# Row statistics of the last 16 tiles moved to ScalarE in an attention layer that streams a 64 MB adjacency matrix

## What is computed

```
h      = relu(layernorm(x))                 # per row: (x - mean) / sqrt(var + 1e-5)
H      = h @ W_fc + b_fc
score  = (H @ a_src)[:, None] + (H @ a_dst)[None, :] + b_att,  -1e9 where adj == 0
out    = x + softmax(score, axis=1) @ H
```

## Time and profile before

| what | value |
|---|---|
| median of 3 runs | 187.31 us (187.17 to 188.09) |
| the profiled execution, its own time | 186.87 us |
| its span, first to last instruction | 185.1 us |
| TensorE busy | 159.5 us, 86% |
| VectorE busy | 132.6 us, 72% |
| ScalarE busy | 63.7 us, 34% |
| DMA | 71.64 MB, mean 387 GB/s |
| granted TensorE clock, mean | 0.972 |

### The profile page before, as it was taken

How to read it: one execution, slowest core, us unless ns; L and a number is a source line. 1 busy time by engine, 2 the same in 40 slices (tenths; PEclk the granted TensorE clock), 3 DMA queues, 4 the chain that set the end, 5 groups by cost and what they waited for, 6 DMA issues and landing times.

```text
span 185.1 us, 2660 instructions
## 1 busy us (share of the span) xinstructions
PE 159.5 (86%) x866; PEld 114.6 (62%) x866; DVE 132.6 (72%) x424; ACT 63.7 (34%) x136; POOL 9.5 (5%) x33
## 2 busy tenths in 40 slices
PE   0509689999955799999999999999999999999970
PEld 0307456675632686867768676686876866877740
DVE  0599999989796996978665487696773625459941
ACT  2353170703604963222232422442242424021020
POOL 2103201300003020000000000000000000000000
PEclk9999969999999799999999999999999999999996
DMA  5999999999999999999999999999999999997112
GB/s 171 384 441 427 425 428 432 430 421 436 420 428 418 439 425 425 436 421 426 420 423 428 428 425 423 425 425 425 426 422 425 438 422 421 418 395 272 70 60 58
DMA packets 8370, 71.64 MB, mean 387 GB/s; under 512 B 929, under 2 KB 1698, under 8 KB 3490
## 3 DMA queue, kind: packets, MB, share of 16 engines
q1 hardware_dynamic: 7776, 71.18, 91.9%
q10 hardware_dynamic: 578, 0.26, 0.6%
HBM read 69.34 MB, written 2.10 MB: 386 GB/s over the span
## 4 chain that ended last, share of the span: by engine, by line
PE 51%; DVE 21%; DMA 21%; ACT 2%; issue 2%; SPq 0%; DVEq 0%
PE bank L807 21%; PE bank L813 19%; DMA ring<-adj 17%; PE bank L831 6%; DVE mask L463 5%; DVE low L486 4%; DMA x_sb<-x 4%; PE bank L855 3%; DVE mask L472 3%; ACT weighted L359 2%; PE bank L845 1%; DVE stats L480 1%; DVE x_sb L594 1%; DVE low L574 1%; DVE x_sb L601 1%
## 5 line engine op out<-in xcount | busy, mean ns | idle before, releaser
L807 PE MATMUL bank<-mask,high 128*128 128x512 f32 x256 | 79.4, 412 | 14.3 <-DVE mask L472 6.9
L463 DVE TENSOR_SCALAR mask<-ring 128x1024 fp32r<-128x1024 int32 (+2 forms) x66 | 59.6, 920 | 29.5 <-DMA ring<-adj 18.2
L813 PE MATMUL bank<-mask,low 128*128 128x512 f32 x256 | 76.4, 401 | 0.0
L807 PEld LDWEIGHTS bank<-mask,high 128*128 128x128 f32 x256 | 47.2, 193 | 33.8 <-issue 8.7
L813 PEld LDWEIGHTS bank<-mask,low 128*128 128x128 f32 x256 | 49.7, 194 | 11.0
L405 ACT ACTIVATE mask<-ring,half_steep 128x512 fp32r<-128x512 int32 x43 | 28.8, 718 | 58.7 <-DMA ring<-adj 38.8
L831 PE MATMUL bank<-mask,w_cols 128*32 128x512 bf16 x256 | 20.3, 402 | 0.0
L371 ACT ACTIVATE relu<-x_sb,neg_mean 128x128 f32<-128x128 f32 x32 | 9.8, 390 | 13.3 <-DVE neg_mean L495 13.3
L831 PEld LDWEIGHTS bank<-mask,w_cols 128*32 128x32 bf16 x256 | 5.9, 96 | 11.4 <-issue 7.2
L480 DVE BATCH_NORM_STATS2 stats<-x_sb 128x6 f32<-128x128 f32 x32 | 7.2, 280 | 6.7 <-DMA x_sb<-x 6.7
L359 ACT ACTIVATE weighted<-relu,w_over_std 128x128 f32<-128x128 f32 x32 | 10.1, 391 | 3.3 <-DVE w_over_std L563 3.2
(11 more groups left out here) (80 smaller groups left out, 61.7 us busy)
## 6 DMA issues: line engine op xcount, KB each, us to landing
ring<-adj SPq DMA_DIRECT2D x18, 2048.0 KB, 16.2
ring<-adj SPq DMA_DIRECT2D x16, 1536.0 KB, 12.5
ring<-adj SPq DMA_DIRECT2D x3, 1024.0 KB, 9.1
out<-x_sb SPq DMA_DIRECT2D x7, 256.0 KB, 13.4
x_sb<-x SPq DMA_DIRECT2D x1, 1024.0 KB, 20.3
ring<-adj SPq DMA_DIRECT2D x4, 256.0 KB, 16.7
x_sb<-x SPq DMA_DIRECT2D x2, 256.0 KB, 5.4
x_sb<-x SPq DMA_DIRECT2D x1, 512.0 KB, 9.8
```

Source lines behind the costliest of these rows:

```text
L463: nc.vector.tensor_scalar(mask[:, n % MASKS, 0:cols], ring[:, n // 2 % RING, begin:begin + cols], 0.0, None, ALU.is_gt).then_inc(masks_rea ...
L807: nc.tensor.matmul(bank[:, b, :], high[:, t, :], mask[:, n % MASKS, cols], start=(t == 0), stop=False)
L813: last = nc.tensor.matmul(bank[:, b, :], low[:, t, :], mask[:, n % MASKS, cols], start=False, stop=(t == T - 1))
```

## The change

- VectorE's first chain of deviations covers tiles 0 to 7 at once (`SPANS`); tiles 8 to 15 keep a chain on VectorE; the four stages of scores and weights stay as they are. SyncE issues the first two loads of x ahead of the first halves of adj.
- For tiles 16 to 31 ScalarE makes the negative means (`late_means`: a copy with scale -1/128 and its accumulator output) and the sums of squared deviations (`late_squares`: a square with the mean as bias and its accumulator output). Each writes 128x128 into `low` or `high` beside the one column that is wanted. VectorE's 16 `bn_stats`, its steps on the halves and the first steps of the chain for these tiles are gone; the chain waits for all 16 squares.
- Dots go into the gaps of their own chain: dots 0 to 3 into the first, 8 to 15 into the second, and dots 16 to 23 with the quarters of mask 12 into the third; dots 24 to 31 follow it.
- Masks are put in another order: 8 to 11 ahead of the third chain, 13 behind the scores of stage 3, 14 to 19 between the splits.

More of the change, by code:

```diff
@@ new lines, in late_means @@
+            def late_means(t0, t1):
[5 more added lines that the diff above has]
+            def late_squares(t0, t1):
+                for t in range(t0, t1):
+                    act.wait_ge(late_means_ready, t - LATE + 1)
+                    nc.scalar.activation(high[:, t, :], x_sb[:, t, :], ACT.Square, bias=neg_mean[:, t:t + 1],
+                                         accum_out=var[:, t:t + 1]).then_inc(squares_ready, 1)
@@ L374, in _, with row_weights_of @@
+            def row_weights_of(k):
+                tiles = slice(*STAGES[k])
+                act.wait_ge(d_ready, k + 1)
+                nc.scalar.activation(w_j[:, tiles], d_raw[:, tiles], ACT.Exp, bias=minus_bound[:]).then_inc(w_ready, 1)
+            act.wait_ge(means_ready, 1)
+            relu_tiles(0, 4)
             act.wait_ge(v_in_psum, 1)
             nc.scalar.copy(v_rows[:].rearrange("p c d -> p (c d)"), ps_v).then_inc(v_rows_ready, 1)
[L376 to L391, removed]
@@ new lines, in _ @@
+            relu_tiles(4, 8)
+            row_weights_of(0)
+            act.wait_ge(w_over_std_ready, 1)
+            weigh(0)
+            weigh(1)
+            take_high(0)
+            weigh(2)
+            take_high(1)
+            act.wait_ge(lines_in_psum, 1)
+            nc.scalar.copy(lines[:], ps_lines).then_inc(lines_ready, 1)
+            take_high(2)
+            row_weights_of(1)
+            act.wait_ge(w_over_std_ready, 2)
+            weigh(3)
+            take_high(3)
+            late_means(16, 20)
@@ new lines, in _ @@
+            act.wait_ge(means_ready, 2)
[12 more added lines that the diff above has]
+            row_weights_of(3)
+            act.wait_ge(w_over_std_ready, 4)
+            for u in range(6, 10):
+                weigh(u)
+                if u > 6:
+                    take_high(u - 1)
@@ L608, in _ @@
             dve.wait_ge(x_landed[0], 16)
-            for t in range(0, 4):
+            for t in range(0, 8):
                 last = stats_of(t)
@@ L615, in _ @@
             nc.vector.tensor_scalar(minus_bound[:], dst_square[:], -HALF_NORM, -HALF_NORM, ALU.mult, ALU.add)
-            scores(0, dot_of(3))
-            mask_quarter(0, 0)
+            scores(0)
+            mask_quarter(0, 1)
             row_weights(0)
-            mask_quarter(0, 1)
             mask_quarter(0, 2)
+            mask_quarter(0, 3)
             split(0)
-            mask_quarter(0, 3)
             split(1)
-            deviations(1, between_1)
+            mask_unit(1)
+            split(2)
             for t in range(4, 8):
@@ L627, in _ @@
             scores(1, last)
[L628 to L632, removed]
+            mask_unit(2)
             row_weights(1)
@@ L636, in _ @@
             mask_unit(4)
+            for t in range(8, 16):
+                last = stats_of(t)
+            link(last)
+            link(sum_of_halves(1))
+            negative_mean(1).then_inc(means_ready, 1)
             mask_unit(5)
-            deviations(2, between_2)
+            deviations(1, between_1)
             scores(2)
```

78 lines of the change are left out of this document (24 added, 54 removed).

## The result

| what | before | changed |
|---|---|---|
| median (7 runs each, on the same chip) | 187.47 us (187.17 to 188.09) | 186.41 us (186.06 to 186.62) |
| ratio | | 0.9938, 95% from 0.9922 to 0.9954 |
| profiled execution, its own time / span | 186.87 / 185.1 us | 186.51 / 184.7 us |
| VectorE busy, instructions | 132.6 us, 424 | 127.2 us, 374 |
| ScalarE busy, instructions | 63.7 us, 136 | 74.5 us, 200 |

The change makes the kernel 0.6% faster, 1.06 us. The forecast was "no change" at 187.3 us: that is wrong. The time lies 0.01 us inside the lower end of the range, 186.4, which is luck.

A forecast was written before the change was run, and what follows sets the result against it. Bound: the landing of units 64 and 65, set by bytes, then 21 us of gapless TensorE. Terms 0 + 0 - 0.12 + 0 gave 186.75 for an execution like the profiled one, 187.3 as median (no change); range 186.4 to 188.8.

The forecast's parts named there:

- The bound: End of the kernel: landing of units 64 and 65 at 154.91, plus 1.3 us, 21 us of TensorE, last rows.
- That landing is a matter of bytes: Landing of units 64 and 65: DMA engines always full at 427 GB/s, bytes ahead unchanged, so loads cost 0.
- One of the signs that I had named for being wrong: Landing of units 64 and 65 moved by more than 1 us with the DMA engines full all along.
- TensorE tied with the landing: At unit 64 TensorE came 0.12 us ahead of the mask, so its earlier work gains at most 0.12 us.
- ScalarE's price: Tiles 16 to 31 on ScalarE: a mean costs 0.40 us and a square 0.50, accumulator read taken as 0.2.
- S: When ScalarE's 16 squares for tiles 16 to 31 are done: 46.6 us, bounds 44.1 to 48.9.
- From S to the end of units 16 to 19: Relus, dots, masks, then TensorE's denominators: done 22.6 us after the squares, at 69.2, 2.2 us ahead of 71.44.
- Lead isn't passed on, lateness is: TensorE leaving units 16 to 19 before 71.44 gains at most 0.12 us; leaving later costs nearly all of it.
- Start, tiles 8 to 15, loads: Three terms worth 0 each: TensorE begins within about 1 us of before; loads cost something past about 50 us.
- ScalarE's chain too long: Slower rival: accumulator reads from 0.31 us delay the squares past 48.9; at 0.42 the time is 189.6; chance 0.11.
- The gain gets through: Faster rival: landings not the bound, TensorE's 2.2 us at unit 16 come off the end, 185.1; chance 0.07.
- The clock: Slower rival: TensorE idles 2.2 us ahead of its last 21 us, slowed clock costs 1.7 us, 189.0; chance 0.04.

The follow-up runs named there:

- experiment 3: The changed kernel without the 12 low-part matmuls of tiles 21 to 23 in group 0: 186.43 us, ratio to before 0.9949.
- experiment 11: The changed kernel with 8 more unused squares on ScalarE ahead of the 16 that count: 186.47 us, ratio to before 0.9951.
- experiment 2: The kernel before without the 12 low-part matmuls of tiles 21 to 23 in group 0: 187.46 us, ratio to before 1.0001.
- experiment 1: The kernel before, unchanged, timed and profiled again: 187.38 us, ratio 0.9997.
- experiment 5: The changed kernel with 52 one-column memsets on VectorE, four a unit at units 40 to 52: 187.31 us, ratio to before 0.9983.
- experiment 6: The changed kernel with 26 one-column memsets on VectorE, two a unit at units 40 to 52: 186.44 us, ratio to before 0.9943.
- experiment 7: The kernel before without the 28 VectorE multiply-adds of row_sum for tiles 4 to 31: 186.99 us, ratio to before 0.9972.
- experiment 10: The kernel before with 36 one-column memsets on VectorE in place of the 28 row_sum multiply-adds: 187.61 us, ratio to before 1.0025.
- experiment 8: The kernel before with only the first two loads of x put ahead of the first halves of adj: 187.31 us, ratio 0.9982.
- experiment 12: The changed kernel with the first loads of x and adj in the order of before: 186.36 us, ratio to before 0.9948.
- experiment 4: The changed kernel with 16 more unused squares on ScalarE ahead of the 16 that count: 188.12 us, ratio to before 1.0038.
- experiment 9: The kernel before without the 28 row_sum multiply-adds and without the 12 low-part matmuls of tiles 21 to 23: 186.32 us, ratio 0.9940.

## Why the prediction was wrong

**The bound: right.** A landing ahead of group 2 ends the wait, with the DMA engines full at 427 GB/s throughout, and 21 us of gapless TensorE stand behind it. Experiments 3 and 11 confirm it for the changed kernel and experiment 2 for the one before.

**"That landing is a matter of bytes": the step that failed.** From it the sum took 0 for the landing. The bytes are the same and the landing came 1.18 us earlier than in experiment 1 and 0.61 earlier than in the profile of before, since its time is that of the bytes plus the lag of the last share, and each of VectorE's instruction fetches ahead of it puts 0.9 to 1.0 us on that lag; the change took one of them out (experiments 5, 6, 7 and 10). The number was in front of me: 0.95 us between 145.37 and 154.91 that the bytes did not explain. I called it unevenness and supposed that the order of the first loads may move it; experiments 8 and 12 say it does not. Looking at the queues in those 9.5 us would have shown the one packet that wasn't adj. Since I had kept it as an uncertainty of 0.95 us, the range just held, by 0.01 us and by luck; the chances did not. One of the signs that I had named for being wrong came true: a landing moved by more than 1 us, measured from experiment 1, with the DMA engines full.

**TensorE tied with the landing: true of one execution.** In the profiled execution it came 0.12 us ahead of the mask, in experiment 1 it waited 0.29. That execution was quicker than all seven timed ones beside it; VectorE's share began in it with a lag of 1.16 us, less than in any other of the 14 profiles (1.33 to 2.28). I built a sum of hundredths on it. The conclusion stood, that an earlier TensorE brings almost nothing as long as the landing stays. But with the landing 1.2 us earlier, TensorE's time counts: it would have ended last, as in experiment 7, and about half the gain would have been lost. So the change needs both of its effects: the fetch, and some of TensorE's 5.1 us.

**ScalarE's price: right in kind, too high in size.** The read of the accumulator lasts 0.19 us but adds only 0.09 to the distance: means 0.29 us apart and squares 0.39, where I took 0.40 and 0.50. By the formula of the Trainium skill (ScalarE: Activation LUTs, section What ACT_TABLE_LOAD costs) they would be about 0.20 and 0.29 apart without the read; the difference to what is measured is again the 0.09, for which the page has no figure. The last five means begin at 35.23, not 36.6, and S came at 42.9 instead of 46.6; the lower end of my bounds gave 44.1.

**From S to the end of units 16 to 19: right, 0.8 us short.** Scores at S + 6.3 (49.19; forecast S + 6.2), TensorE done at S + 23.4 (66.30; forecast S + 22.6). With S itself 3.7 us early, the lead at unit 16 was 5.1 us instead of 2.2.

**Lead isn't passed on, lateness is: right.** The wait of 0.70 at unit 30 and 0.71 at unit 64 show the lead lost; experiment 11 gives 4.6 us of it away for nothing; experiment 4 ends 1.07 us behind before at unit 16 and 0.74 us behind it in time, although its mask 64 began 1.1 us earlier than in experiment 1.

**Start, tiles 8 to 15, loads: right, worth nothing.** The first matmul came at 12.18 instead of 14.15, 2 us earlier where I had said within 1, and none of it is left at unit 30. The loads run dry when S passes 50, I said; in experiment 4 S was 49.24 and they had just done so.

**The rivals.** ScalarE's chain too long: no; experiment 4 shows the mechanism with its price, and experiments 11 and 4 put the point from which it costs between 4.6 and 6.2 us of TensorE's time at unit 16 from where the change left it. The gain gets through: the sign was right and the mechanism wrong, 1.06 us instead of 2.2, and not TensorE's. The clock: granted 1.00 in the 21 us of group 2, so it did not occur.

**Settled by the shares.** That a fetch delays one share, that a load has landed with its last share, and that the lag stays while the DMA engines are full, is what the 16 times of each load show in all 14 profiles. Fetches put down to ScalarE (8192 bytes) moved one lag by 0.65 to 0.70 us where they can be told apart from TensorE's, those of TensorE (16384 bytes) by 1.4 to 1.6 us. They do cost a landing something where their share becomes the last: TensorE's at 65.5 us in before put 0.45 us on all landings until VectorE's share overtook it again. What decides mask 64 is how often one and the same share is hit: VectorE's is hit three times behind 20 us in before, and TensorE's four fetches from 65 to 133 us hit four different ones. The profiles of before and changed differ by 0.4 us at mask 10 (40.08 in experiment 1, 39.68 changed), but there another share is the last, at 1.95 and 1.59 us, and VectorE's overtakes it; that difference is no part of the 1.18 us.

**Open.** Why a packet of 8192 bytes, whose record lasts 0.325 us, costs its share 1 us, and ScalarE's of the same size 0.7, is not settled, nor why the lags begin where they do. That a share is the work of one of the 16 DMA engines is inferred; the trace has no name of an engine. That a packet belongs to VectorE rests on the counts, and now also on its hitting the same share each time. The Trainium skill (Runtime: NRT & Kernel Launch, section Instruction fetch mechanics) has each sequencer fetch its own instructions by DMA in blocks of 16 KiB at a cost "mostly hidden"; the packets of q8 agree with the size, those of q14 are half of that, and with full DMA engines experiments 5 and 6 put 0.87 us on one of them, so here the measurement decides.

No version was faster than the changed kernel: experiments 3, 9 and 12 lie within 0.1 us of it.

## What to carry to other kernels

- Where loads bound a kernel with full DMA engines, follow the landings one by one. An interval that is longer than its bytes is a term of the sum and not noise; look at what else is in the queues there. Two causes can fall into one interval: where the trace gives the shares of a load, follow each share's lag and not the last one alone. Count instructions as well as busy time: 26 tiny ones cost nothing and 52 cost 0.9 us, because a fetch slid in front of the last landing that counts.
- When two things end at nearly the same time, one alone brings little and both together bring all (0.0, 0.55 and 1.03 us here). Test them apart and together.
- Compare the profiled execution with the timed runs before building on its tenths; where it lies outside of them, its ties may not be typical.

## What the runs showed of the hardware that was not expected

- With the DMA engines at a share of 1.01, each instruction fetch of 8192 bytes put down to VectorE delayed one and the same of a load's 16 shares by 0.9 to 1.0 us, for this and all later loads, and left the other 15 where they were; the landing moves by as much as that share gets behind the last of the others (0.2 to 1.0 us in the fetches from 50 us on).
- Fetches put down to ScalarE (8192 bytes) cost another share 0.65 to 0.70 us, those of TensorE (16384 bytes) 1.4 to 1.6 us; most of them never show in a landing.
- The lags begin anew when the loads run dry: in experiment 4 the last was 1.89 us ahead of a stretch with a DMA share of 0.80 and 1.34 behind it.
- ScalarE's accumulator output costs 0.09 us on a 128x128 tile, although its read is shown with 0.19 us: the two overlap.
- 26 memsets of one column on VectorE with time to spare cost nothing that can be measured (186.44 against 186.41); with 52 the loss of 0.87 us is of the size of the one fetch that they bring.
